# Attention block kernel on one core: products beside value products as four 32-column tiles, transposes first

## The reference

```python
x = _layernorm(x + _L0_attn_ref(x, ...))          # stage 0: causal self-attention
x = _layernorm(x + _L0_xattn_ref(x, ctx, ...))    # stage 1: attention to a context, a key mask
x = _layernorm(x + _L0_ffn_ref(x, ...))           # stage 2: causal attention, then 4 dense experts, top 2
x = _layernorm(x + _L1_attn_ref(x, ...))          # stage 3: attention with rotary positions
x = _layernorm(x + _L1_xattn_ref(x, ctx, ...))    # stage 4: a mask, and weights multiplied by group_prob
x = _layernorm(x + _L1_ffn_ref(x, ...))           # routed mixture: 8 experts, top 1, capacity 320
```

## Time and profile before

| | |
|---|---|
| median of 3 runs | 1508.32 us (1502.15 to 1515.01) |
| the profiled execution: time | 1505.13 us |
| its span | 1503.4 us |
| TensorE busy | 1430.2 us, 95% of the span, 11096 matmuls |
| mean granted TensorE clock | 0.968 |

### The profile page before, as it was taken

The page is one execution under the profiler, slowest core; times in us unless marked ns, Lnnn a source line. Parts: engine busy times, 40 slices in busy tenths (PEclk is TensorE's granted clock), DMA queues, the critical chain, the costliest instruction groups (busy, mean ns, idle before and its releaser), DMA issues. The chain is left out here.

```text
span 1503.4 us, 29009 instructions
## 1 busy us (share of the span) xinstructions
PE 1430.2 (95%) x11096; PEld 1077.9 (72%) x11096; DVE 994.6 (66%) x2109; ACT 877.6 (58%) x1442; POOL 558.5 (37%) x727
## 2 busy tenths in 40 slices
PE   8999999999989999999999999999999999868997
PEld 5667656666668888888888888865655555437997
DVE  4677777766674455464544534587778989856896
ACT  1455667666646565564645646454547767637775
POOL 4246765613331111321312112152223554442766
PEclk9899999999979999999999999998999999988999
DMA  7689776754450203201010010124765643106451
GB/s 153 100 146 183 148 158 118 136 102 61 67 71 2 43 2 57 36 16 44 2 43 24 21 50 1 44 75 112 135 158 105 118 90 66 38 32 211 143 178 63
DMA packets 100200, 125.98 MB, mean 84 GB/s; under 512 B 7900, under 2 KB 90083, under 8 KB 97504
## 3 DMA queue, kind: packets, MB, share of 16 engines
q1 hardware_dynamic: 96496, 118.84, 38.4%
q0 software_dynamic: 1984, 4.09, 0.8%
q10 hardware_dynamic: 1584, 1.20, 0.3%
HBM read 50.96 MB, written 9.51 MB: 40 GB/s over the span
## 5 line engine op out<-in xcount | busy, mean ns | idle before, releaser
L950 ACT ACTIVATE probs<-eslot 128x1024 f32<-128x1024 f32 x188 | 192.6, 1024 | 110.0 <-PE eslot L682 106.6
L1174 DVE TENSOR_REDUCE mx<-mslot 128x4 f32<-128x1024 f32 x128 | 156.4, 1222 | 108.7 <-PE mslot L653 107.3
L1473 POOL TENSOR_SCALAR_AFFINE_SELECT probs<-probs 128x512 f32<-128x512 f32 x128 | 82.6, 646 | 352.3 <-ACT probs L948 351.7
L653 PE MATMUL mslot<-stack 48*128 48x256 f32 (+2 forms) x1110 | 166.2, 338 | 8.7 <-DVE mx L1174 5.9
L653 PEld LDWEIGHTS mslot<-stack 48*128 48x128 f32 (+1 forms) x1110 | 99.3, 191 | 96.9 <-issue 76.6
L1168 DVE TENSOR_REDUCE mx_blocks<-mslot 128x3 f32<-128x384 f32 x214 | 114.7, 554 | 60.3 <-PE mslot L653 44.9
L948 ACT ACTIVATE probs<-eslot 128x512 f32<-128x512 f32 (+1 forms) x256 | 111.7, 490 | 43.5 <-PE eslot L682 43.1
L697 PE MATMUL bank<-probs,v 128*32 128x256 f32 (+1 forms) x2048 | 133.0, 373 | 2.2 <-ACT slot_rows_sb L973 0.8
L1412 POOL TENSOR_SCALAR ave<-amv 128x2 f32<-128x2 f32 x64 | 22.7, 355 | 293.1 <-DVE amv L1086 252.4
L682 PE MATMUL eslot<-stack 50*128 50x256 f32 (+1 forms) x1264 | 125.3, 276 | 5.0 <-ACT probs L950 2.4
L745 PE MATMUL bank<-slot_rows_sb,l 128*128 128x256 f32 x512 | 114.8, 382 | 0.0
(11 more groups left out here) (277 smaller groups left out, 3488.7 us busy)
## 6 DMA issues: line engine op xcount, KB each, us to landing
stack<-split SPq DMA_DIRECT2D x192, 256.0 KB
w<-in_w SPq DMA_DIRECT2D x16, 1024.0 KB, 6.2
stack<-split SPq DMA_DIRECT2D x96, 128.0 KB
slot_rows_sb<-in_proj SPq DMA_DIRECT2D x15, 256.0 KB, 3.8
slot_rows<-hTf SPq DMA_DIRECT2D x4, 650.0 KB, 4.5
slot_rows_sb<-slot_rows SPq DMA_DIRECT2D x4, 650.0 KB, 5.2
expert_rows<-slot_rows SPq DMA_DIRECT2D x8, 260.0 KB, 2.7
hT<-in_xT SPq DMA_DIRECT2D x8, 256.0 KB, 9.5
```

Source lines behind the costliest of these rows:

```text
L653: mm = pe.matmul(ps[:, first:first + m], queries(u, h, k)[:, qt * P:(qt + 1) * P], keys(u, h, k)[:, 0:m], start=clear, stop=clear or qt == ...
L950: e = act.activation(PR[:, k, :, :, :].rearrange("p a k q -> p (a k q)"), ps[:, :, :, :].rearrange("p a k q -> p (a k q)"), ACT.Exp, scale ...
L1174: dve.tensor_reduce(MX[:, :, :, p].rearrange("p q a -> p a q"), MSLOT[0][:, :, :].rearrange("p a (q k) -> p a q k", q=TT), AX.X, ALU.max)\
L1473: pool.affine_select(diagonal, diagonal, [[0, 2 * TT], [1, P]], ALU.is_ge, 0.0, base=0, channel_multiplier=-1)\
```

## The change

1. `beside_columns(order)` collects every step of a stretch between score products in which a `mix`, `shift` or `sums` stands (NARROW). In these steps each full product is issued as four products of 32 weight columns, into the four quarters of the output's partitions, by a helper `product`. Transposes, the products of split operands (units 2 to 7: q, k, v), `spread` and the warm-up products stay as they are.
2. Transposes (`T`, `TC`, `y0`, `y1`, `yT`, `Tf`, `xT`) get a rank of their own, TURNS = 4.5, ahead of OTHER in their slot.
3. Some entries of PLACE move: in stage 0 `x high`, `x low` -11 to -13, `q` -10 and `q end` -9 to -12, `k` -9 and `k end` -8 to -10, `v` -5 and `v end` -3 to -6; in stage 1 `T` -11 to -12; in stage 2 `Tf` 27 to 28; in stage 3 `v end` -2 to -3 and `yT` 23 to 22; in stage 4 `yT` 23 to 22; in stages 0 to 3 `y1` 21 to 20.

```diff
+COLUMNS = P // 4
-ENDS, MASK, EXP, TRIM, MAX, WEIGHT, OTHER, MIX = 0, 1, 3, 4, 2, 6, 5, 7
+ENDS, MASK, EXP, TRIM, MAX, WEIGHT, OTHER, MIX, TURNS = 0, 1, 3, 4, 2, 6, 5, 7, 4.5
+TURNED = ("T", "TC", "y0", "y1", "yT", "Tf", "xT")
...
-            put(at(n), OTHER, step, u, 0)
+            put(at(n), TURNS if step in TURNED else OTHER, step, u, 0)
...
+def beside_columns(order):
+
+    narrow, run, columns = set(), [], False
+    for at, (step, u, n) in enumerate(order):
+        if step in ("max", "exp"):
+            narrow.update(run if columns else ())
+            run, columns = [], False
+        else:
+            run.append(at)
+            columns = columns or step in ("mix", "shift", "sums")
+    return narrow
...
+        def product(out, left, right, start, stop, **kwargs):
+
+            for r in range(0, P, wide[0]):
+                mm = pe.matmul(out[r:r + wide[0]], left[:, r:r + wide[0]], right, start=start, stop=stop, **kwargs)
+            return mm
...
-                mm = pe.matmul(bank_of(kind, u)[:, co, :], WEIGHT_OF[kind][:, ci, at], src[:, ci, :],
+                mm = product(bank_of(kind, u)[:, co, :], WEIGHT_OF[kind][:, ci, at], src[:, ci, :],
                                start=ci == 0, stop=ci == CC - 1)
...
-        for step, u, n in ORDER:
+        for at, (step, u, n) in enumerate(ORDER):
             l = layer(u)
+            wide[0] = COLUMNS if at in NARROW else P
```

More of the change, by code:

```diff
@@ L136, in schedule @@
     PLACE = (
[3 rows of a table removed]
[3 rows of a table added]
          "k": -9, "k end": -8, "mask": -7, "xb": -7, "mask row": -7, "stack": -6, "v": -5, "v end": -4, "shift": 8,
[1 row of a table removed]
[1 row of a table added]
         {"H": -19, "T": -18, "q": -16, "q end": -15, "k": -14, "k end": -14, "sums": -11, "spread": -10, "split": -7,
[2 rows of a table removed]
[2 rows of a table added]
          "e3b": 32, "e2c": 33, "down3": 34, "e1a": 35, "e1b": 35, "down2": 35, "down1": 36, "normf": 39},
         {"H": -19, "T": -18, "xb": -17, "q": -14, "q end": -14, "k": -14, "k end": -14, "swap": -13, "split": -7,
[1 row of a table removed]
[1 row of a table added]
          "norm": 31},
         {"keys": -17, "masks": -16, "T": -13, "q": -10, "q end": -10, "k": -9, "turn masks": -8, "k end": -8,
-         "stack": -8, "xb": -7, "v": -4, "v end": -2, "group": 1, "shift": 8, "y0": 21, "y1": 21, "yT": 23, "w": 25,
+         "stack": -8, "xb": -7, "v": -4, "v end": -2, "group": 1, "shift": 8, "y0": 21, "y1": 21, "yT": 22, "w": 25,
          "w end": 26, "norm": 30, "even": 30, "xT": 30, "even rows": 31, "logits": 32, "chances": 32, "rank": 33,
@@ L378, in attention_layers @@
     ORDER = schedule()
+    NARROW = beside_columns(ORDER)
     def bank_of(*label):
@@ L483, in _ @@
         filling = set()
+        wide = [P]
         def bank(*label):
@@ L567, in project_rows @@
                     continue
-                mm = pe.matmul(bank_of(kind, u)[:, tt, :], src[:, ci, at], WEIGHT_OF[kind][:, ci, :],
+                mm = product(bank_of(kind, u)[:, tt, :], src[:, ci, at], WEIGHT_OF[kind][:, ci, :],
                                start=ci == 0, stop=ci == CC - 1)
@@ L629, in mask_for_max @@
                 if l == 4:
-                    pe.matmul(ps, ident_b[:, :], NQ[u % RING][:, :, :], start=True, stop=False)
+                    product(ps, ident_b[:, :], NQ[u % RING][:, :, :], start=True, stop=False)
                 else:
-                    pe.matmul(ps.rearrange("p (n k) -> p n k", k=P)[:, 0:2 * TT:2, :], ident_b[:, :],
+                    product(ps.rearrange("p (n k) -> p n k", k=P)[:, 0:2 * TT:2, :], ident_b[:, :],
                               causal_q[:, :].unsqueeze(1).to_broadcast([P, TT, P]), start=True, stop=False,
@@ L639, in mask_for_exp @@
             for a in range(2):
-                pe.matmul(ps[:, a, :, :], ident_b[:, :], NK[u % RING][:, :, :], start=True, stop=False)
+                product(ps[:, a, :, :], ident_b[:, :], NK[u % RING][:, :, :], start=True, stop=False)
         def scores_for_max(u, p):
@@ L744, in expert @@
                     for k in range(kc):
-                        mm = pe.matmul(ps[:, j, :], w[:, k, o:o + P], src[:, k, :], start=k == 0, stop=k == kc - 1)
+                        mm = product(ps[:, j, :], w[:, k, o:o + P], src[:, k, :], start=k == 0, stop=k == kc - 1)
                 mm.then_inc(*bank_filled(kind, u, part))
@@ L751, in expert_down @@
                 for k in range(4):
-                    mm = pe.matmul(ps[:, tt, 0:KEEP], src[:, k, tt * P:(tt + 1) * P], downs[:, e, k, :],
+                    mm = product(ps[:, tt, 0:KEEP], src[:, k, tt * P:(tt + 1) * P], downs[:, e, k, :],
                                    start=k == 0, stop=k == 3)
@@ L829, in _ @@
                     for ci in range(CC):
-                        mm = pe.matmul(ps[:, tt, 0:E1], HTF[:, ci, tt * P:(tt + 1) * P], wg[:, ci, :],
+                        mm = product(ps[:, tt, 0:E1], HTF[:, ci, tt * P:(tt + 1) * P], wg[:, ci, :],
                                        start=ci == 0, stop=ci == CC - 1)
@@ L842, in _ @@
                     for k, counted in enumerate(earlier):
-                        pe.matmul(ps[:, tt, 0:E1], ones_b[:, :], counted, start=k == 0, stop=False)
-                    mm = pe.matmul(ps[:, tt, 0:E1], upto_b[:, :], OH[:, g, :], start=not earlier, stop=True)
+                        product(ps[:, tt, 0:E1], ones_b[:, :], counted, start=k == 0, stop=False)
+                    mm = product(ps[:, tt, 0:E1], upto_b[:, :], OH[:, g, :], start=not earlier, stop=True)
                 mm.then_inc(*bank_filled("rank", u))
@@ L854, in _ @@
                     for ci in range(CC):
-                        mm = pe.matmul(ps[:, tt, 0:4], HTF[:, ci, tt * P:(tt + 1) * P], gate[:, ci, :],
+                        mm = product(ps[:, tt, 0:4], HTF[:, ci, tt * P:(tt + 1) * P], gate[:, ci, :],
                                        start=ci == 0, stop=ci == CC - 1)
```

## The result

The changed kernel takes 1569.34 us (median of 4 runs, 1568.41 to 1572.72), the one before 1511.66 us beside it (4 runs): ratio 1.0394, 95% interval 1.0337 to 1.0451. The forecast was 1476, the end of its range 1503.

What follows compares the result with a forecast made beforehand. TensorE's own instructions, busy 95% of the span, were taken as the bound. Gross savings of 40.9 us, with +5.5, +2.5, -3.2, -3.0, -1.0 and +8.1 given back, made -32.0 us: 1476 us, range 1458 to 1503.

Steps and rivals of the forecast that it cites:

- q, k and x high/low of stage 0, two slots earlier: Stage 0: these steps issue no transfer and their readers have idle time; nothing, a little gain at the start.
- v, +5.5: Stage 0, units 3 to 7: VectorE's earlier v read waits for value products, +1.1 us each, 5.5 in all.
- Tf in slot 28: Stage 2, unit 16: TensorE's 3.23 us wait mostly goes, -3.2 us, and the low clock with it, -3.0.
- The other moves: Remaining moved steps: work only goes from one slot into the next and readers are half idle; nothing.
- Changes of mode: TensorE, all stages: 282 fewer changes of the array's use at 0.094 us each, 26.5 us saved.
- heads: TensorE: 129 fewer W runs beginning behind scores with an f32 product, 0.104 us each, 13.4 us saved.
- give-back: Stages 0, 1 and 4: a third of 24.2 us saved turns into waiting for other engines, +8.1 us.
- Narrow sets at full pace: TensorE: four narrow instructions take as long as one full product of 256 columns, 0.217 us; no cost taken.
- TC: Stage 1, units 8 to 10: TC ahead of q waits 0.85 us longer for GpSimd, +2.5 us.
- Rival 1: Stages 0, 1 and 4: VectorE and GpSimd set the pace, gain mostly given back; 8 us gained, 1500; chance 0.20.
- Rival 2: Stages 1 to 3: transposes in a row lower the granted clock; about 1558, or 1517 with half the falls; chance 0.04.
- Rival 3: Experts' long runs: four tiles don't keep pace, 0.396 us a set instead of 0.216; about 1720; chance 0.03.

Runs made afterwards that it cites:

- b1: e1 with Tf of stage 2 in slot 28 instead of 27: 1509.46 us, ratio 1.0009 to the kernel before.
- e1: The changed kernel with the table PLACE and ranks of the kernel before, so only the narrow products: 1497.29 us, ratio 0.9932 to the kernel before.
- e3: The changed kernel with stage 0's row of PLACE as before: 1527.46 us, ratio 1.0133 to the kernel before.
- s1_v: The kernel before with only v and v end of stage 0 moved to slot -6: 1521.64 us, ratio 1.0111.
- c1: e1 with q end of stage 0 in slot -8 instead of -9: 1505.66 us, ratio 0.9982 to the kernel before.

## Why the prediction was wrong

*"q, k and x high/low of stage 0, two slots earlier ... Nothing, and a little gain at the start."* The step that failed most: +29 alone. I looked for transfers that these steps issue and for idle time of their readers (ScalarE 69 of 117 us busy). Both are true and neither asks for what a reader waits. The reader's buffer is freed by a transfer, and the trace of before had that wait already, 1.6 to 2.2 us in each of units 4 to 7. That is only 7 of ScalarE's 48 idle us in this stretch: how idle a reader is doesn't say how early it can go.

*v, +5.5 (bounds 0 and 17).* The right mechanism, mis-sized: +13. A wait has the size forecast, but there are two to a unit, 9.0 us in all instead of 5.5; the price through the clock was left out, though I had priced that for Tf.

*"Tf in slot 28", -6.2 with the clock.* Wrong in sign: +12 (b1 over e1). I counted the wait ahead of Tf, which is a single one in unit 16, and not who follows it: gate, in each of eight units. Even that single wait only moved: after, TensorE waits 2.92 us for a maximum at 487.00, and the granted clock is 0.50 from 488 to 494. Of the -6.2, the -3.0 for the clock was a choice within its bounds, and nothing of it came in the kernel after.

*"The other moves: nothing, the work goes from one slot into the next", and the ranks.* Together with Tf 30 us. Three transposes' steps at the head of a slot take some 1.5 us and leave three reads to VectorE and ScalarE. Whichever step comes next waits for them: down1 for a bank, gate for rows, the next score for a maximum. Before, Tf stood a slot earlier, and down1's 2.7 us of products (581.25 to 583.95) came between it and gate and covered its read.

*Changes of mode -26.5 and heads -13.4.* The direction held, and the narrow products alone gain; of some 17 and 23 us for their share of the changes 11 and 16 arrived. Stage 0's 25 fewer changes gave nothing, stage 4's 105 gave 3 to 4 us of 10 (reads of y, e1 against before; one execution of each). No run takes the heads apart from the changes. The give-back was forecast at a third in three stages; it is over half in these two.

*Narrow sets at full pace: held* (0.2175 us). The Trainium skill (TensorE: Matmul & The Clock Gate, section "Wait — 56ns, not 53.3ns?" in Part 1) states a floor of about 62 ns per matmul with the hardware decoder off; here 64 matmuls passed in 3.48 us, 54 ns each, so that floor did not bind.

*TC, +2.5 (0 to 7).* Waits at the transposes for qk are 5.9 us in three, before 0.8 in two: some 5 more, within its bounds.

*The rivals.* None had this. Rival 1 has the right kind, "waits like that of v are several", at 8 us. Rival 2's mechanism, a clock that falls because transposes stand in a row, did not occur in stage 2: twelve stand in a row at 625.36, and from 510 to 960 us the clock is 1.00. In stages 1 and 3 the clock is 0.98 and 0.91, before 0.96 and 0.93. The Trainium skill (the same page, Part 4: PE-mode transpose), by which they don't count as busy for the clock gate, would have spoken for it. Rival 3 is excluded by the sets' pace. Of the signs I named, TensorE's waits for maxima did grow by more than 20 us (16.4 to 38.8).

The sum in medians: narrow products -11, stage 0 +34, order of stages 1 to 4 +30, together 53 of the 61 that after has over the 1508 of these runs. Taken in the order before, e1, e3, after, the steps are -11, +30 and +42: stage 0's row costs 8 us more in the new order than its four moves cost in the old one. That row also holds `y1` in slot 20; whether it or the combination makes the 8 was not tested.

## What to carry to other kernels

A step moved earlier is priced by its reader: ask what frees the buffer that the reader writes, and follow that once round to the next unit; where hold plus transfer already equals the time of a unit, going earlier lengthens the unit, however idle the engines look (here three slots earlier made the hold, and the unit, 7.5 us longer). When producers are put side by side to save TensorE time, look for the longer work that used to lie between a producer and its consumer, since it was the cover of the reader's latency. A change in how products are issued and a change in their order are worth testing apart: here the one gained 0.7%, and the other lost over six times as much and hid it.

## What the runs showed that I had not expected

Short waits may cost more than their length. In s1_v some 9 us of waits for maxima in stage 0 came with a mean granted clock of 0.82 instead of 1.00 over 117 us, and 13 us in the result. A clock of 0.50 stood right behind 1.19 and 0.99 us of waiting, for some 13 us. No run shows that the waits alone lower it; c1 waits hardly more than e1 from 60 to 164 us (6.0 for 5.4 us) and has 0.95 to 0.96 where e1 has 1.00.

Making four of each of some 2170 instructions and of their weight loads (29009 to 42025 instructions in all; the prediction had counted 2132) costs TensorE nothing that these runs can tell. In e1 the weight load's busy time even fell, from 1077.9 us to:

```profile
PE 1406.3 (94%) x17505; PEld 981.4 (66%) x17510; DVE 992.1 (67%) x2109; ACT 876.4 (59%) x1442; POOL 558.7 (37%) x727
```
